# Reordering the passage from the context loop to the feed-forward of a Perceiver layer: group sums ahead of batch products, the fourth batch with the third, one normalisation of all eight tiles

## What is computed

```python
x = x + xattn(layernorm(x), ctx, ctx)      # focused linear attention, 16 heads of 16
x = x + attn(layernorm(x))                 # qkv, running sum over rows, gate
x = x + ffn(layernorm(x))                  # NVFP4 fake-quantised linears, 256 -> 1024 -> 256
# xattn: q, k through Wq, Wk, focused (softmax of 3*log|.|, times the row mean) and the
#   top 11 of 16 of each head kept; kv = k^T v per head and batch; y = q kv / (q mean(k)); y Wp^T
# attn:  q, k, v = split(x W_qkv^T + b); state = cumsum(k * v, rows)
#   return q * state * sigmoid(x W_gate^T + b_gate)
# ffn:   every x and w quantised in blocks of 16: e4m3 scales, e2m1 values
```

## Time and profile before

| | us |
|---|---|
| median of 3 runs | 470.62 (470.41 to 471.29) |
| the profiled execution | 470.4 |
| its span in the trace | 468.7 |
| DVE busy in the span | 447.6 (96%) |
| PE busy | 386.4 (82%) |
| ACT busy | 360.4 (77%) |

### The profile page before, as it was taken

One profiled execution on the slowest core, in us unless ns is written; L12 is line 12 of the kernel. 1 busy time (PEld: TensorE's weight loads), 2 busy tenths in 40 slices (PEclk: granted clock), 3 DMA queues, 4 the chain that ended last, 5 costly groups with the idle time before them and its releaser, 6 DMA issues.

```text
span 468.7 us, 6040 instructions
## 1 busy us (share of the span) xinstructions
PE 386.4 (82%) x1931; PEld 306.3 (65%) x1934; DVE 447.6 (96%) x685; ACT 360.4 (77%) x950; POOL 6.2 (1%) x22
## 2 busy tenths in 40 slices
PE   7986758989989998998997997991999899648567
PEld 6775547877877876886785885891987445314334
DVE  6999999999999999999999999999998889899995
ACT  2679997997997997997888978885438678666765
POOL 2001000000000000000000000000000000000000
PEclk9999879999999999999999999997799999956968
DMA  6990000320220220230140040022020000000001
GB/s 224 348 324 2 1 1 1 97 82 2 90 90 2 91 90 1 68 113 1 46 134 1 28 132 22 2 92 88 1 90 1 0 1 1 0 0 1 22 23 46
DMA packets 27071, 27.66 MB, mean 59 GB/s; under 512 B 1184, under 2 KB 26784, under 8 KB 27040
## 3 DMA queue, kind: packets, MB, share of 16 engines
q1 hardware_dynamic: 26736, 27.27, 18.2%
q0 software_dynamic: 160, 0.01, 0.0%
q10 hardware_dynamic: 144, 0.00, 0.0%
HBM read 26.22 MB, written 1.05 MB: 58 GB/s over the span
## 4 chain that ended last, share of the span: by engine, by line
DVE 86%; PE 6%; ACT 4%; issue 2%; DMA 1%; SPq 0%; DVEq 0%
DVE mask L1405 8%; DVE focus_words L1325 8%; DVE focus_words L1305 8%; DVE sorted L1361 4%; DVE merge L1374 4%; DVE sorted L1362 4%; DVE level L1331 4%; DVE level L1332 4%; DVE sorted L1234 3%; DVE amax L1203 2%; DVE sorted L1367 2%; DVE sorted L1366 2%; DVE keymax L1364 2%; DVE merge L1372 2%; DVE rank L1385 2%
## 5 line engine op out<-in xcount | busy, mean ns | idle before, releaser
L817 PE MATMUL bank<-WkT,rows_T 128*128 128x256 f32 x512 | 123.8, 388 | 29.4 <-ACT rows_T L434 29.4
L817 PEld LDWEIGHTS bank<-WkT,rows_T 128*128 128x128 f32 x512 | 94.3, 192 | 46.2 <-ACT rows_T L434 35.2
L909 PE MATMUL bank<-ctx_words,focus_words 128*128 128x257 f32 x512 | 115.3, 383 | 2.8 <-ACT focus_words L533 2.8
L909 PEld LDWEIGHTS bank<-ctx_words,focus_words 128*128 128x128 f32 x512 | 99.5, 197 | 15.1 <-ACT focus_words L533 4.4
L521 ACT ACTIVATE focus_words<-focus_words,shift,ff 128x256 f32<-128x256 f32 x136 | 79.8, 590 | 0.6
L487 ACT ACTIVATE focus_words<-bank 128x256 f32<-128x256 f32 x136 | 50.1, 382 | 25.7 <-PE bank L817 25.7
L533 ACT ACTIVATE focus_words<-focus_words,row_scale 128x256 f32<-128x256 f32 x136 | 56.2, 515 | 11.3 <-DVE row_scale L1318 11.3
L434 ACT ACTIVATE rows_T<-bank 128x512 f32<-128x512 f32 x78 | 44.3, 595 | 17.1 <-PE bank L790 16.9
L790 PE MATMUL bank<-ident,ctx_words 128*128 128x128 f32 x256 | 37.5, 275 | 3.8 <-DMA ctx_words<-in_ctx_dram 3.5
L1405 DVE TENSOR_TENSOR mask<-focus_words,fifth 128x2048 bf16<-128x2048 f32 x17 | 39.0, 2292 | 0.5
L790 PEld LDWEIGHTS bank<-ident,ctx_words 128*128 128x128 f32 x256 | 31.0, 142 | 11.7 <-DMA ctx_words<-in_ctx_dram 6.2
(11 more groups left out here) (207 smaller groups left out, 589.3 us busy)
## 6 DMA issues: line engine op xcount, KB each, us to landing
ctx_words<-in_ctx_dram SPq DMA_DIRECT2D x32, 512.0 KB, 3.9
ctx_words<-in_L_ffn_gate_w_dram SPq DMA_DIRECT2D x2, 1024.0 KB, 6.7
ctx_words<-in_L_ffn_up_w_dram SPq DMA_DIRECT2D x2, 1024.0 KB, 8.2
xs<-in_x_dram SPq DMA_DIRECT2D x4, 256.0 KB, 5.0
ctx_words<-in_L_ffn_down_w_dram SPq DMA_DIRECT2D x2, 512.0 KB, 10.7
ctx_words<-in_L_ffn_down_w_dram SPq DMA_DIRECT2D x1, 1024.0 KB, 4.8
out_dram<-xs SPq DMA_DIRECT2D x3, 256.0 KB, 2.1
gateT<-in_L_attn_W_qkv_dram SPq DMA_DIRECT2D x1, 512.0 KB, 7.0
```

The source lines that it names most:

```text
L817: ins = pe.matmul(proj_bank[m][:, t * D:(t + 1) * D], rows_T[:, m % 2, 2 * t + k, :], WT[:, k, :], start=(k == 0), stop=(k == KT - 1))
L909: ins = pe.matmul(sum_bank[k][:, 0:GW], heads_half(expo[slot][:, t, :], k), ctx_ring[:, s, t, :], start=(s == 0 and t == 0), stop=(s == PE ...
```

## The change

- PE, last pair: sum_group(15) moves ahead of mix(0) and mix(1); project_out(0), project_out(1) and mixed_quad(2) move behind sum_group(16).
- PE, tail: mixed_quad(2), project_out(0), sums_quad(3), project_out(1), key_values(3), project_out(2), mix(3), mixed_quad(3), project_out(3), and only then the quads of the normalised rows and gate_tile(0). mix(3) uses the banks of project_out(0) and (1) (mix_bank) and so waits for the second attn_added, not the third; running(0) now carries the wait for all four attn_added.
- Normalisation: NORM_TILES has one second normalisation of all eight tiles; ACT normalises the tiles 0 to 3 after it and 4 to 7 behind gate_tile(1). One guess and two table loads less on ACT; the table of the sigmoid is loaded ahead of normalise.
- DVE: weight_reciprocals and scale_weight(0) stand ahead of add_batch(0); mix(3) and add_batch(3) are moved up, ahead of the one mean_variance(1); cut_to_code(1) lies between that and refine_for_act(1); scale_weight(2) comes ahead of the clip of weight 1; gate_tile(0) comes after weight 1, gate_tile(1) after weight 2.
- ACT: spread_weight(0) and (1), save_sums and half_step(0) are moved up accordingly.

```diff
--- before.py
+++ after.py
@@ -193,7 +193,7 @@
         gated_sum = ring_part(3, 512, 512).rearrange("p (s c) -> p s c", s=2)
         zr = rank[:, :, :, :].rearrange("p t s c -> p (t s c)")[:, 0:T * HEADS].rearrange("p (t k h) -> p t k h", t=T, k=KT)
         kv_bank = [proj_bank[0][:, 0:D], proj_bank[0][:, D:2 * D], proj_bank[1][:, 0:D], proj_bank[3][:, 0:D]]
-        mix_bank = (proj_bank[2:4], proj_bank[0:2], proj_bank[2:4], proj_bank[2:4])
+        mix_bank = (proj_bank[2:4], proj_bank[0:2], proj_bank[2:4], proj_bank[0:2])
         attn_bank = proj_bank
         rows_bank = (quad_bank[0], oct_bank[1])
         last_rows = flat(plane[5])[:, 0:2 * 512].rearrange("p (n b c) -> p n b c", n=2, b=4)
@@ -286,7 +286,7 @@
 
 
         EVERY, LOWER, UPPER = slice(0, T), slice(0, T // 2), slice(T // 2, T)
-        NORM_TILES = (EVERY, LOWER, UPPER, LOWER, UPPER)
+        NORM_TILES = (EVERY, EVERY, LOWER, UPPER)
 
 
 
@@ -296,7 +296,7 @@
             return QK_QUADS + rest + PAIRS * n + m
 
         AFTER_QUAD = group_quad(CGROUPS + 1, 0)
-        TAIL_QUADS = ("sums0", "sums1", "sums2", "mixed0", "mixed1", "mixed2", "sums3", "xhat0", "xhat1", "mixed3",
+        TAIL_QUADS = ("sums0", "sums1", "sums2", "mixed0", "mixed1", "mixed2", "sums3", "mixed3", "xhat0", "xhat1",
                       "xhat2", "xhat3")
         TAIL_ROWS = {"sums0": rows_T[:, 0], "sums1": rows_T[:, 1], "sums2": rows_T[:, 0],
                      "mixed0": rows_T[:, 1], "mixed1": rows_T[:, 0], "mixed2": rows_T[:, 1],
@@ -466,10 +466,10 @@
                 act.wait_ge(astep, astep_n[0])
                 act.activation(rstd0[:, tiles], ln_var[:, tiles], ACT.Exp, scale=-0.5).then_inc(rstd0_ready, 1)
 
-            def normalise(k, dst, cols=D):
+            def normalise(k, dst, cols, tiles):
 
                 act.wait_ge(norm_ready, k)
-                for t in range(T)[NORM_TILES[k]]:
+                for t in tiles:
                     act.activation(dst[:, t, 0:cols], xs[:, t, 0:cols], ACT.Identity, scale=rstd[:, t:t + 1],
                                    bias=shift_ln[:, t:t + 1]).then_inc(x_hat_ready, 1)
 
@@ -702,34 +702,31 @@
 
             tail_rows_to_sbuf("mixed0", (kv_in_psum, 2))
             tail_rows_to_sbuf("mixed1", (kv_in_psum, 3))
+            spread_weight(0)
+            spread_weight(1)
+            save_sums(BATCH)
             tail_rows_to_sbuf("mixed2", (attn_in_psum, 1))
+            tail_rows_to_sbuf("sums3", None)
+            half_step(0, slice(0, T * D))
+            spread_weight(2)
+            tail_rows_to_sbuf("mixed3", None)
+            half_step(1, slice(0, T * D))
             rstd_guess(1)
-            normalise(1, x_hat2, D - 1)
             act.preload_act_table_set(SIGMOID)
-            save_sums(BATCH)
-            tail_rows_to_sbuf("sums3", None)
+            normalise(1, x_hat2, D - 1, FORE_TILES)
             tail_rows_to_sbuf("xhat0", (attn_in_psum, 2))
             tail_rows_to_sbuf("xhat1", (attn_in_psum, 3))
-            half_step(0, slice(0, T * D))
-            spread_weight(0)
+            half_step(2, slice(0, T * D))
             gate_tile(0)
-            spread_weight(1)
-            half_step(1, slice(0, T * D))
             gate_tile(1)
-            tail_rows_to_sbuf("mixed3", None)
-            act.preload_act_table_set(NAT_LOG_EXP)
-            spread_weight(2)
-            rstd_guess(2)
-            act.preload_act_table_set(SIGMOID)
-            normalise(2, x_hat2, D - 1)
+            normalise(1, x_hat2, D - 1, HIND_TILES)
+            tail_rows_to_sbuf("xhat2", (qkvg_in_psum, 2))
             gate_tile(2)
-            tail_rows_to_sbuf("xhat2", (qkvg_in_psum, 2))
             gate_tile(3)
             tail_rows_to_sbuf("xhat3", (qkvg_in_psum, 4))
-            half_step(2, slice(0, T * D))
             gate_tile(4)
             act.preload_act_table_set(NAT_LOG_EXP)
-            rstd_guess(3)
+            rstd_guess(2)
             act.preload_act_table_set(SIGMOID)
             gate_tile(5)
             weight_oct(0, 0)
@@ -744,7 +741,7 @@
             gate_tile(7)
             rows_oct(0)
             act.preload_act_table_set(NAT_LOG_EXP)
-            rstd_guess(4)
+            rstd_guess(3)
             act.preload_act_table_set(SILU)
             silu_half(0)
             silu_half(1)
@@ -878,7 +875,7 @@
                 if m == 2:
                     pe.wait_ge(mixed_ready, 2)
                 if m == 3:
-                    pe.wait_ge(attn_added, 3)
+                    pe.wait_ge(attn_added, 2)
                 for t in (2 * m, 2 * m + 1):
                     for k in range(KT):
                         ins = pe.matmul(mix_bank[m][t % 2][:, k * KVW:(k + 1) * KVW], qT[:, t, k, :], kv[:, m, k, :],
@@ -955,15 +952,12 @@
                                            two_tiles(att_rows[part - 1] if part else out_rows, r))
                 if last:
                     key_values(2)
+                    sum_group(a)
                     mix(0)
                     mix(1)
-                    sum_group(a)
                     mixed_quad(0)
                     mix(2)
                     mixed_quad(1)
-                    project_out(0)
-                    project_out(1)
-                    mixed_quad(2)
                     sum_group(CGROUPS)
                 else:
                     sum_group(a)
@@ -978,7 +972,7 @@
             def running(t):
 
                 pe.wait_ge(kv_prod_ready, t + 1)
-                if t == 1:
+                if t == 0:
                     pe.wait_ge(attn_added, PAIRS)
                 if t >= 2:
                     pe.wait_ge(running_added, t - 1)
@@ -1077,26 +1071,28 @@
                     ins = pe.matmul(dst, hid_fp4T[:, t % 2, k, :], downT[:, k, :], start=False, stop=(k == HIDDEN // P - 1))
                 ins.then_inc(down_in_psum, 1)
 
-            project_out(2)
+            mixed_quad(2)
+            project_out(0)
             pe.wait_ge(sums_saved, BATCH + 1)
             sums_quad(3)
+            project_out(1)
+            key_values(3)
+            project_out(2)
+            mix(3)
+            mixed_quad(3)
+            project_out(3)
             xhat2_quad(0)
             xhat2_quad(1)
-            key_values(3)
             pe.wait_ge(bias_row_ready, 16)
             gate_tile(0)
-            mix(3)
             gate_tile(1)
-            mixed_quad(3)
             running(0)
-            project_out(3)
             gate_tile(2)
             running(1)
-            gate_half(3, 0)
             xhat2_quad(2)
-            gate_half(3, 1)
+            gate_tile(3)
+            xhat2_quad(3)
             running(2)
-            xhat2_quad(3)
             gate_tile(4)
             running(3)
             gate_tile(5)
@@ -1612,35 +1608,37 @@
             mix(1)
             weight_scales()
             mix(2)
-            add_batch(0)
-            add_batch(1)
-            mean_variance(1)
-            refine_for_act(1)
             weight_reciprocals()
             dve.wait_ge(ffn_loaded, 48)
             scale_weight(0)
-            add_batch(2)
+            add_batch(0)
+            add_batch(1)
             key_values(3)
             weight_codes(0)
+            mix(3)
+            add_batch(2)
             scale_weight(1)
+            add_batch(3)
+            mean_variance(1)
+            cut_to_code(1)
+            refine_for_act(1)
+            scale_weight(2)
+            clip_q()
+            settle()
+            finish_weight(1)
             gate_tile(0)
-            mix(3)
+            dve.wait_ge(ffn_w_ready, 2)
+            weight_codes(2)
             gate_tile(1)
-            weight_codes(1)
             run(0)
-            add_batch(3)
-            mean_variance(2)
-            refine_for_act(2)
-            scale_weight(2)
             gate_tile(2)
             run(1)
             gate_tile(3)
             run(2)
-            weight_codes(2)
             gate_tile(4)
             run(3)
-            mean_variance(3)
-            refine(3)
+            mean_variance(2)
+            refine(2)
             normalise_rows(LOWER)
             gate_tile(5)
             settle()
@@ -1657,8 +1655,8 @@
             gate_tile(7)
             run(6)
             run(7)
-            mean_variance(4)
-            refine(4)
+            mean_variance(3)
+            refine(3)
             normalise_rows(UPPER)
             hidden(0)
             hidden(1)
```

## The result

| | us |
|---|---|
| before, median, on the same chip | 470.96 (470.41 to 471.98) |
| changed kernel, median of 4 runs | 480.06 (476.97 to 481.87) |
| ratio, 95% interval | 1.0182 (1.0151 to 1.0214) |
| predicted | 478.9 (475.0 to 481.5) |

The change costs 9 us (480.06 less 470.96). The runs of the changed kernel also lie 4.9 us apart, where those of the kernel before lie within 1.6. The profiled execution is the slowest of them, 481.87 us with a span of 480.1; what it shows is the loss at its largest.

A forecast was written before the change was run, and what follows sets the result against it. DVE was taken to bound the kernel, with PE only just hidden. 470.4 us plus 5.0 for the queue, 3.3 for the clock and 0.2 for median over profile gave 478.9 us, range 475.0 to 481.5.

The forecast's parts named there:

- Step 1: PE's last pair: sum_group(16) begins at 341.2, 5.2 us earlier; mix(0) ends later, at no cost to DVE.
- Step 2: DVE from 345.77 to the one normalisation: every input is there in time and the shift ends at 366.1.
- Step 3: Gate stage: PE's gate tiles make the lower half's mean_variance 5.0 us later; DVE waits some 10 us.
- Step 4: Behind the gate stage: the order is the old one, nothing takes the delay back, the shift goes to the end.
- Step 5: PE's holes halve its clock: 2.5 us for the long hole, 0.8 for shorter ones; 3.3, between 0 and 5.6.
- The faster one, DVE-bound: Rival: DVE bounds the gate stage; without its two largest waits (3.6 us) and second normalisation (1.3), 465.7 us; chance 0.06.
- No clock loss: Rival: PE's holes are filled by small work or end sooner, only the queue's 5.0 is paid: 475.6 us; chance 0.12.
- All holes: Rival: both shorter PE holes also drop the clock, 5.6 us with the queue's 5.0: 481.2 us; chance 0.06.
- No change: Rival: the 5 us come back in the tail, from DVE idle time behind 391; chance 0.02.

The follow-up runs named there:

- the half gate tiles: Changed kernel with its three PE holes filled by idle matmuls and each gate tile given two matmuls for four: 467.41 us, ratio 0.9919.
- the single fillings: Two runs of the changed kernel with idle matmuls in some PE holes: only the last filled, 478.71 us; only the first two filled, 477.09 us.
- the order with two halves: Changed kernel with its second normalisation again in two halves, gate tiles 0 and 1 back under DVE's weight work: 472.65 us in 10 runs, ratio 1.0042.

## Why the prediction was right, and where it was not

Step 1, sums earlier: right in place, not in time. sum_group(16) came at 343.64, 1.5 us later than the 341.2 of the walk when the 0.9 us that this execution started later is taken off, and took 8.34 instead of 7.12 us, both for the half clock behind the first hole. That mix(0) would be ready for DVE held.

Step 2, DVE's queue up to the normalisation: the queue was right and the inputs were late. DVE's shift came at 371.09, not at 366.1; the forecast had named this mark, more than 2 us late, as a sign that the step is wrong, by a late input, project_out(3) first of all. It was that and project_out(0) and (1): 4.0 us of waits (1.68, 0.69 and 1.64), and 0.9 of this execution's later start. With the holes filled they vanish: the eight aggregations then start 19.5 us behind mix(2) (365.16 less 345.62), where the walk had 19.6 (364.0 less 344.43). So this miss is the clock's and not the order's.

Step 3, the gate stage: right. The walk's difference of 5.0 us for the queue measured 4.84 with the clock held at full, and the half gate tiles, 7.30 us off the yardstick, put it on PE. Waits of 3 us or more were forecast at gate tiles 0, 2 and 4: they are 4.79, 3.65 and 2.30, the last one short of it, with 0.94 at gate tile 3.

Step 4, nothing is given back later: right, 81.6 us against 81.6.

Step 5, the clock: right that it would fall behind the holes and cost time, wrong in its division, and lucky in its sum. At the medians the clock costs 3.3 us (480.06 less 476.79), which is the forecast; but neither median lies near a run. The changed kernel's runs lie at 477.0, 478.8, 481.3 and 481.9, those with filled holes at 475.5 and 478.05, and the profiled one of the upper level lost 1.6 us at the kernel's end and started 1.2 us late. In the profiles the three holes cost 5.7 us, a little over the 5.6 of the upper bound, so that the lower half's mean_variance came at 398.5, beyond the 391 to 397 that I gave. I took 2.5 us for the long hole and 0.8 for the two short ones, on the ground that they were shorter than any hole that the rows showed to matter. By the single fillings it is the other way round: 1.4 us for the hole of 5.2 us, 3.5 for the holes of 2.7 and 2.6. What stands behind the short holes on PE, sum_group(16) with project_out(0) and (1) after it, and the last project_out, is what add_batch waits for.

The rivals. The faster one, DVE-bound, fell with the half gate tiles. Its 465.7 stood on the two rows, of whose 3.6 us only 2.1 lie ahead of 387.05; DVE's waits there for codes and kv, which it left out, are another 2.1, so its price is hardly changed. It was the one that a rule of the Trainium skill, "Perfetto Trace Analysis", section "Identifying the Most-Contended Engine", would have made: weight loads were busy for 5.42 of 10 us. For the old order the rule's answer holds: halving its gate tiles left the yardstick where it was. For the new order the same measure says nearly the same, 11.75 of 23 us between 377 and 400, and there it misleads: halving the gate tiles took 7.3 us off. Matmul occupancy does not tell the two orders apart either (10.00 of 10 us, 23.00 of 23); DVE's busy share does (9.02 of 10 us, 12.09 of 23), and the half gate tiles decide. "No clock loss" at 475.6 is what the run with all three holes filled comes to in its two lower runs (475.40, 475.55). "All holes" at 481.2 is what two of the changed kernel's four runs are (481.29, 481.87); the profile of the slowest shows half clock behind all three holes. I gave it 0.06, which was too little. "No change" found no place where the time could come back, and none was seen.

## What to carry to other kernels

Before two partial steps are merged into one, list what runs under the first of them today: by the walk, two normalisations cost DVE 1.3 us more than one, but the first of them let 7 us of another engine's work start early. Where two engines are nearly balanced, walk both queues with durations from the trace; an order that frees the one can hand the end to the other. And a reordering that makes TensorE wait can have a second price in its clock; filling the holes with idle matmuls tells that price from the queue's. Where the runs of a kernel fall on levels, compare the passage from trace to trace, for a difference of medians can be off by the 2 us that it was here.

## What the runs showed of the hardware that was not expected

The granted clock fell to 1.2 GHz at holes shorter than the 9.88 and 3.65 us of the earlier trace rows: in the run with the last hole filled it was 0.50 in 341 to 343, behind a hole of 2.73 us, and in 361 to 367, behind one of 2.61; in the order with two halves it was 0.50 in 358.8 to 362, behind one of 2.34, and gate tile 0 took 4.63 us. Not every such hole does it: in that same execution one of 2.22 us (337.4 to 339.6) left the clock at 1.00. The Trainium skill, "TensorE: Matmul & The Clock Gate", section "HAM oscillation — how this bites in real kernels", describes the pattern, a matmul kernel whose waits between bursts drop the clock again and again. These traces agree with that pattern, with the durations above; the waits here are for DVE and ACT, those that the skill tells of are for DMA.

How far this explains the spread of the runs is open. In the changed kernel the mean granted clock fits it: 0.932 in the runs of 481.87 and 481.29 us, 0.943 in those of 478.84 and 476.97. In the order with two halves it does not: 0.938 at 471.42 us, 0.939 at 476.84. That filling the holes drew the runs of that order together, from 5.4 to 0.9 us, speaks for the clock; but the two sets were taken on different chips.

The clock also falls outside the changed passage: with the passage kept at full clock, the last 16 matmuls of one execution took 3.07 us for 1.91, at 0.50. The 1.2 us that the same execution lost ahead of mix(2) arise in its first 19 us, where the first 48 transposes took 8.57 us for 7.06 in the kernel before; the granted clock reads 1.00 there in both, so their cause is not shown.
